# Two layers and a third sum over a graph: one group of every second pass of the third sum counted by source node on TensorE, and ScalarE's tile of each last full pass gathered

## The chip, the cores and the metric

The kernel runs on 1 core of one Trainium2 chip. The time is that of the device in microseconds (us). The kernel before took 9507.16 us, the median of 3 runs (9503.04 to 9524.47).

## The reference, cut to what matters

There are 12500 nodes with 128 features, and 212500 edges (100000 random ones in both directions and one self loop for each node), sorted by destination. Each edge has one of 8 relations. Three sums over the edges follow each other, each on the rows that the one before made possible:

```python
def rgcn(x, W, SW, b):                       # W: 8 matrices of 128 x 128
    msg = einsum('nd,rde->rne', x, W)[rel, src]
    return relu(segment_sum(msg, dst) + x @ SW + b)
x1 = layernorm(x + rgcn(rgcn(x, w1, sl1, b1), w2, sl2, b2))      # sums one and two
feat = relu(x1 @ W1 + b1)
h = feat * d_invsqrt                          # d_invsqrt from the in-degrees
agg = segment_sum(h[src], dst)                # sum three: no relation, no matrix
out = layernorm(x1 + (feat - agg * d_invsqrt) @ W2 + b2)
```

What is computed in sum three is, for each destination node n, the sum over its edges of the row h[src]. The result is 12500 x 128 in float32.

## The kernel before, in words

The edge list is cut into 1661 tiles of 128 edges (a tile has one edge for each of the 128 partitions). Seven tiles (KG) are a group, and since the edges are sorted by destination, a group's destinations lie in a window of GN = 64 nodes. Two groups are a pair, and four pairs (p = 0 to 3), so 56 tiles, are a pass, i. There are IT = 29 full passes (0 to 28) and a rest of 37 tiles in three pairs (LEFT) in each sum.

For a tile, the 128 source rows (512 bytes each) are brought into the tile `rows`, which has room for one pass. Three engines do this. GpSimd takes 54 of the 56 tiles with one indirect DMA each (L808). SyncE and ScalarE bring one tile each, the last two of pair 3 (`OWN`), with one small DMA for each of the 128 rows (L867), whose addresses they load 16 at a time from a list in SBUF (`load_own`, L863); the list itself is fetched each pass (L846). In pass 0 ScalarE's tile is gathered by GpSimd too.

TensorE then adds up a group: in sum three one matmul for each tile, of the rows by a one-hot matrix S of 128 x 64 that VectorE makes from the destinations (`one_hot`, L1228), into PSUM (L1211; float32, which is two weight loads and two matmuls for each tile). VectorE adds the 64 columns to the accumulator `acc` (L1255). In sums one and two the one-hot also tells the relation, and a mix with the 8 matrices follows (L980).

The order is tied together so. TensorE ends a pair and raises `summed`. ScalarE's `take` (L771) waits for it, copies the next pass's indices of that pair, and GpSimd may gather them. In a pass of ScalarE (`indices_and_own`) the order in its one queue is: its rows of lists 1 to 3 (48 rows), `take` of pair 0, 32 rows, `take` of pair 1, 32 rows, `take` of pair 2, `take` of pair 3, the wait for the end of the pass on TensorE (`own_free`), and the 16 rows of the next pass's list 0. SyncE's tile of a pass may begin when TensorE has ended the pass before, since it uses the same place in `rows`; then come its 128 rows.

When the sums of 512 nodes are complete (25 chunks in 29 passes), the chunk's tail is run at the end of the pass (`Tail3`): TensorE multiplies (L1708), VectorE normalizes, with a square root on ScalarE between (L1718, which waits for VectorE's variance, and VectorE's next instruction waits for the root, L1748), and SyncE loads (L1288) and stores (L1693) rows and waits for the store. The tail stands in each engine's queue between two passes. Loops run on the engines with register values; the passes belonging to a chunk come from a table.

In the places that the change touches: `Gathers.run` (GpSimd's passes), `wait_rows` (TensorE's waits), `indices_and_own` (ScalarE), `plain_sum` (sum three) and the tiles of `Tail3`.

## Time and profile before

| | us |
|---|---|
| median of 3 runs | 9507.16 |
| the profiled execution's own time | 9512.93 |
| span of its profile, first to last instruction | 9511.2 |
| GpSimd's gathers of sum three (L808), busy | 1504.7 |
| TensorE's matmuls of sum three (L1211), busy | 745.3 |
| VectorE, busy over all | 1975.7 |

Busy times are those of an engine's own instructions; instructions that only issue a DMA, load a register, branch or wait are not counted as busy. A line of a timeline gives the start, the length of a merged stretch of like instructions, the engine, line, operation and operands, how many they were, and in brackets how long the engine had been idle and what ended that. SPq and ACTq are the DMA issues of SyncE and ScalarE, PEld are TensorE's weight loads. Sum three runs from about 6497 us to the end.

### The profile page before, as it was taken

Reading aid. Unit: us, or ns where it says so; the run is one execution under the profiler, and the core shown is the slowest. Engines: PE = TensorE matmul, PEld = TensorE weight load, DVE = VectorE, ACT = ScalarE, POOL = GpSimd, SP = SyncE. Lnnn points to the kernel's source line nnn. Section 1 sums busy time; section 2 is a strip of 40 time slices with the busy share of each in tenths; the row PEclk is TensorE's granted clock in tenths of the full one; section 3 lists DMA queues with packets and bytes.
Section 4 is the critical chain, followed back from the end, with each engine's and each line's share of the span. In section 5 each row is a group of like instructions: output and inputs, shape, how many; then the busy total and the mean of one; then the engine's idle time right before and its main releaser. Section 6 shows DMA issues by size and latency. Waiting matters only on the chain.

```text
span 9511.2 us, 99977 instructions
## 1 busy us (share of the span) xinstructions
PE 3350.8 (35%) x13625; PEld 2381.6 (25%) x13626; DVE 1975.7 (21%) x3147; ACT 130.3 (1%) x430; POOL 4561.2 (48%) x4822
## 2 busy tenths in 40 slices
PE   3333433434333434344343343344222222222223
PEld 2222222222222322222222222224222222222223
DVE  4322332323232212122121221122001001001001
ACT  0000000000000000000000000000000000000000
POOL 4545444444444444444544444444554454455454
PEclk6666666666666666666666666665555555555555
DMA  1111111111111111111111111111111111111111
GB/s 49 40 40 42 36 38 40 41 39 39 38 43 41 36 40 44 40 40 42 40 47 40 40 41 40 46 42 35 40 42 39 40 42 40 37 43 41 37 43 39
DMA packets 239445, 385.74 MB, mean 41 GB/s; under 512 B 106473, under 2 KB 137532, under 8 KB 239100
## 3 DMA queue, kind: packets, MB, share of 16 engines
q0 software_dynamic: 153984, 315.67, 12.7%
q1 hardware_dynamic: 61768, 60.65, 2.1%
q10 hardware_dynamic: 23348, 6.44, 0.3%
q14 instruction: 326, 2.67, 0.1%
q8 instruction: 19, 0.31, 0.0%
HBM read 356.60 MB, written 25.75 MB: 40 GB/s over the span
## 4 chain that ended last, share of the span: by engine, by line
SPq 49%; issue 37%; ACTq 8%; PE 3%; DMA 1%; DVE 1%; another core or an unknown queue 0%; ACT 0%; DVEq 0%
SPq L867 38%; ACTq L867 7%; SPq L863 6%; ACTq L863 1%; PE bank L1008 1%; SPq L684 1%; SPq L686 1%; SPq L846 1%; SPq L683 1%; PE bank L980 0%; SPq L109 0%; SPq L850 0%; SPq L856 0%; PE bank L1565 0%
## 5 line engine op out<-in xcount | busy, mean ns | idle before, releaser
L808 POOL DMA_INDIRECT rows<-x_d,idx x1590 | 1504.0, 946 | 1687.7 <-ACT idx L771 1202.7
L808 POOL DMA_INDIRECT rows<-in_x_dram,idx x1604 | 1518.1, 946 | 1651.4 <-ACT idx L771 1186.7
L808 POOL DMA_INDIRECT rows<-h_d,idx x1583 | 1504.7, 951 | 1505.4 <-ACT idx L771 1026.0
L1008 PE MATMUL bank<-r_S,rows 128*128 128x128 f32 x6644 | 1115.6, 331 | 2023.5 <-DMA rows<-in_x_dram 998.4
L1008 PEld LDWEIGHTS bank<-r_S,rows 128*128 128x128 f32 x6644 | 1058.0, 242 | 2083.9 <-issue 2062.0
L1211 PE MATMUL bank<-r_S,rows 128*128 128x64 f32 x3322 | 745.3, 411 | 2093.9 <-DMA rows<-h_d 1479.7
L1211 PEld LDWEIGHTS bank<-r_S,rows 128*128 128x128 f32 x3322 | 733.6, 328 | 2108.1 <-issue 2107.4
L1104 DVE COPY r_agg<-bank 128x512 f32<-128x512 f32 x476 | 320.5, 687 | 2969.1 <-PE bank L1008 2059.7
L1255 DVE TENSOR_TENSOR acc<-acc,bank 128x64 f32 x238 | 52.7, 222 | 2093.2 <-issue 962.4
L1046 DVE TENSOR_TENSOR r_S<-bank,key 128x1792 f32<-128x1792 f32 x238 | 479.0, 2013 | 0.7 <-issue 0.7
L980 PE MATMUL bank<-r_agg,w1s 128*128 128x512 f32 (+1 forms) x512 | 448.5, 1044 | 42.5 <-DVE r_agg L1104 24.1
L980 PE MATMUL bank<-r_agg,w2s 128*128 128x512 f32 (+1 forms) x512 | 448.3, 1044 | 35.2 <-DVE r_agg L1104 21.3
L992 PE MATMUL bank<-zeros_bf 128*128 128x512 bf16 x476 | 223.5, 470 | 594.3 <-DVE r_agg L1104 483.8
L1044 DVE TENSOR_REDUCE r_placed<-r_hot 128x192 bf16<-128x1344 bf16 x119 | 291.0, 2445 | 4.1
L1090 DVE TENSOR_TENSOR acc<-acc,bank 128x64 f32 x476 | 105.7, 222 | 799.6 <-issue 352.9
L992 PEld LDWEIGHTS bank<-zeros_bf 128*128 128x128 bf16 x476 | 52.6, 110 | 674.2 <-DVE r_agg L1104 506.7
L980 PEld LDWEIGHTS bank<-r_agg,w1s 128*128 128x128 f32 x512 | 122.8, 251 | 323.9 <-issue 323.6
L980 PEld LDWEIGHTS bank<-r_agg,w2s 128*128 128x128 f32 x512 | 123.4, 253 | 315.9 <-issue 315.6
L1041 DVE TENSOR_TENSOR r_hot<-bank,b_spot 128x1344 bf16<-128x1344 f32 x119 | 185.3, 1557 | 18.2 <-issue 6.3
L771 ACT COPY idx<-src_i 128x14 int32 x360 | 72.6, 203 | 7419.9 <-issue 6032.1
L1361 PE MATMUL bank<-ident,d_zr 128*128 128x128 f32 x98 | 27.5, 435 | 321.5 <-DVEq L1636 321.5
L1228 DVE TENSOR_TENSOR r_S<-bank,key 128x896 f32<-128x896 f32 x119 | 129.8, 1092 | 35.8 <-DVE acc L1255 27.7
(157 smaller groups left out, 1357.9 us busy)
## 6 DMA issues: line engine op xcount, KB each, us to landing
rows<-in_x_dram SPq DMA_DIRECT2D x3712, 0.5 KB
rows<-x_d SPq DMA_DIRECT2D x3712, 0.5 KB
rows<-h_d SPq DMA_DIRECT2D x3712, 0.5 KB
rows<-in_x_dram ACTq DMA_DIRECT2D x3584, 0.5 KB
rows<-x_d ACTq DMA_DIRECT2D x3584, 0.5 KB
rows<-h_d ACTq DMA_DIRECT2D x3584, 0.5 KB
rows<-in_x_dram,idx POOLq DMA_INDIRECT x1604
rows<-x_d,idx POOLq DMA_INDIRECT x1590
```

The lines of the kernel that those rows point to most:

```text
L808: pool.indirect_dma_start(out=self.c.rows[:, self.place(s), :], out_offset=None, in_=self.table[:, :], in_offset=bass.IndirectOffsetOnAxis ...
L863: _, starts = nc.values_load_multi_w_load_instructions(c.list_i[o][0:1, first:first + LIST], engines=bass.OrderedEngineSet([eng.engine]), ...
L867: eng.dma_start(to[row:row + 1, :], table[bass.ds(start, ROW)].unsqueeze(0)).then_inc(self.own[o][row // (P // OWN_SEMS)], 16)
L980: mm = pe.matmul(mix_ps[:, 0:groups * GN], W[:, r, :], agg[:, h0:h0 + groups, :, r], start=(r == 0), stop=(r == NREL - 1))
L992: pe.matmul(agg_ps[j][:, :], c.zeros_bf[:, :], c.zeros, start=True, stop=False, skip_group_check=True)
L1008: mm = pe.matmul(agg_ps[j][:, bass.ds(offs[j * KG + k], TK)], c.rows[:, g.place(h * KG + k), :], S[:, pb, j * KG + k, :], start=False, sto ...
L1041: ch.then(dve.tensor_tensor(hot[:, b, :, :], spots.unsqueeze(1).broadcast_to([P, PT, SPOTS]), bc_last(blocks.spot[:, at], SPOTS), ALU.is_e ...
L1044: dve.tensor_reduce(placed[:, b, :, :], hot[:, b, :, :].rearrange("p (j k) n -> p j n k", k=KG), AX.X, ALU.add)
L1046: dve.tensor_tensor(S[:, b, :, :], c.iota[:, :].unsqueeze(1).broadcast_to([P, PT, TK]), bc_last(c.key[:, at], TK), ALU.is_equal).then_inc( ...
L1104: dve.tensor_copy(agg[:, h, :, :], agg_ps[h % BUFS][:, :].rearrange("p (n r) -> p n r", r=NREL)).then_inc(agg_out, 1)
L1211: mm = pe.matmul(sum_ps[b][:, j * GN:(j + 1) * GN], c.rows[:, g.place(h * KG + k), :], S[:, b, j * KG + k, :], start=(k == 0), stop=(k == ...
L1228: dve.tensor_tensor(S[:, p % BUFS, :, :], c.iota[:, 0:GN].unsqueeze(1).broadcast_to([P, PT, GN]), bc_last(c.key[:, bass.ds(i * UN + p * PT ...
```

## The change

In every even pass from 2 to 28 of sum three, group 6 (`DENSE`, the first group of pair 3, 7 tiles) is no longer gathered. In its place the table h (12544 rows with padding, 6.4 MB) is kept in SBUF, loaded by 13 DMAs at the start of the sum from ScalarE's queue. It is cut into 13 units of 1024 rows (the last has 256). For a unit, VectorE makes a one-hot of the place of each edge's source within the unit (`pair_hot`, 128 x 896, bf16) and TensorE multiplies it with a one-hot of the partition (`part_hot`), which counts, for each source row of the unit and each of the 64 destinations, how many edges there are (`count`: one matmul of zeros and 7 of bf16, into a PSUM bank of 512 columns). VectorE copies the counts out, and TensorE multiplies the unit's 8 blocks of table rows with them (`mult`: 8 float32 matmuls of 128 x 64, the counts read with a stride of 8), all into one bank, `dense_ps`, which VectorE adds to the accumulator in place of the gathered group. The 26 steps on TensorE (`PE_ENDS`) and 27 on VectorE (`DVE_ENDS`) for one such group are spread over the two passes before its place: after the pairs 0 to 3 of the odd pass (4, 4, 4 and 3 steps on TensorE, 7, 4, 4 and 3 on VectorE), and after pairs 0 to 2 of the even pass (4, 4 and 3; 4, 4 and 1). GpSimd's loop of sum three holds two passes, an odd and an even one.

In all three sums, ScalarE brings no rows in the last full pass (28); its tile is gathered by GpSimd. The tiles `key` and `relf` are bf16. `Tail3`'s tiles share room. Sum three takes its number of rounds and its table of windows from the same entry as the others.

The diff, cut to its core:

```diff
+DENSE = RING - 2
+DENSE_TILES = range(DENSE * KG, DENSE * KG + KG)
...
+def ends_of(i):
+
+    return (i + (ENDING - (IT - 1))) >> ENDING_BITS
...
-            iteration(q, 0, FULL, skip, first=True)
-            with pool.Fori(1, IT) as i:
-                iteration(q, i, FULL)
+            iteration(q, 0, FULL, skip, OWN[:BY_ACT])
+            if self.then:
+                with pool.Fori(1, IT - 1) as i:
+                    iteration(q, i, FULL, others=OWN)
+                iteration(q, IT - 1, FULL, others=OWN[:BY_ACT])
+            else:
+                with pool.Fori(0, IT // 2 - 1) as n:
+                    i = pool.snap(n * 2)
+                    iteration(q, i + 1, FULL, others=OWN)
+                    iteration(q, i + 2, FULL, others=(*DENSE_TILES, *OWN))
+                iteration(q, IT - 2, FULL, others=OWN)
+                iteration(q, IT - 1, FULL, others=(*DENSE_TILES, *OWN[:BY_ACT]))
             iteration(q, IT, LEFT)
...
-                pe.wait_ge(self.landed[h], i * (gathered * 16) + (gathered + 1) * 16)
+                pe.wait_ge(self.landed[h], i * (gathered * 16) + ends_of(i) * 16 + (gathered + 1) * 16)
...
-    with act.If(i > 0):
+    with act.If(i > ends * IT):
         g.load_own(nc, act, BY_ACT, own[:-4])
+    act.end_ifs()
+    with act.If(i > IT - 2):
+        g.list_there(act, BY_ACT, q, i)
+        for share in g.own[BY_ACT]:
+            act.sem_inc(share, P // OWN_SEMS * 16)
     act.end_ifs()
     for p in range(PR):
         g.take(act, p, q, i + 1)
         if p < PR // 2:
-            with act.If(i > 0):
+            with act.If(i > ends * IT):
                 g.load_own(nc, act, BY_ACT, own[-4:][2 * p:2 * p + 2])
             act.end_ifs()
         if p == PR // 2:
             g.fetch_list(act, BY_ACT, i + 1)
-    with act.If(i < IT - 1):
+    with act.If(i < IT - 2):
...
+        for u in range(UNITS):
+            act.dma_start(table[:, u * NREL:u * NREL + rows_of(u), :],
+                          g.table[u * AT_UNIT:u * AT_UNIT + P * rows_of(u), :].rearrange("(p r) f -> p r f", r=rows_of(u))
+                          ).then_inc(table_in, 16)
...
+            def dense(half, np, p, before):
+
+                made = steps_before(q, half, DVE_STEPS)
+                _, offs = nc.values_load_multi_w_load_instructions(
+                    c.off_i[0:1, bass.ds(half * (2 * PR) + DENSE // PAIR, 1), 0:KG], engines=bass.OrderedEngineSet([pe.engine]),
+                    min_val=0, max_val=(GN - TN) * NREL, skip_runtime_bounds_check_because="clamped on the chip")
+                order = [(count_done(u), 0, u) for u in range(UNITS)] + [(mult_done(u), 1, u) for u in range(UNITS)]
+                for _, kind, u in sorted(order)[part(PE_ENDS, p, before)]:
+                    if kind == 0:
+                        pe.wait_ge(from_dve, made + hot_done(u))
+                        pe.matmul(count_ps[u % 2][:, :], c.zeros_bf[:, :], c.zeros, start=True, stop=False,
+                                  skip_group_check=True)
+                        for k in range(KG):
+                            mm = pe.matmul(count_ps[u % 2][:, bass.ds(offs[k], TK)], part_hot[:, k, :],
+                                           pair_hot[u % 2][:, k, :], start=False, stop=(k == KG - 1),
+                                           skip_group_check=True)
+                    else:
+                        pe.wait_ge(from_dve, made + copy_done(u))
+                        if u == 0:
+                            pe.wait_ge(added, np + BUFS)
+                            pe.wait_ge(table_in, UNITS * 16)
+                        of = counts[u % 2].rearrange("p (n r) -> p n r", r=NREL)
+                        for r in range(rows_of(u)):
+                            mm = pe.matmul(dense_ps, table[:, u * NREL + r, :], of[:, :, r],
+                                           start=(u == 0 and r == 0), stop=(u == UNITS - 1 and r == LAST_ROWS - 1))
+                    mm.then_inc(from_pe, 1)
...
+                        if h == DENSE:
+                            def gathered(to):
+                                for k in range(KG):
+                                    pe.matmul(to, c.rows[:, g.place(h * KG + k), :], S[:, b, j * KG + k, :],
+                                              start=(k == 0), stop=(k == KG - 1))
+                                gate(pe, c.passed)
+
+                            with pe.If(i < 1):
+                                pe.wait_ge(g.landed[h], KG * 16)
+                                gathered(dense_ps)
+                            pe.end_ifs()
+                            with pe.If(i < half * 2):
+                                pe.wait_ge(g.landed[h], i * (KG * 8) + KG * 24)
+                                gathered(sum_ps[b][:, j * GN:(j + 1) * GN])
+                            pe.end_ifs()
+                            continue
...
+                    if part is FULL:
+                        with pe.If(i < half * 2):
+                            dense(half, np, p, True)
+                        pe.end_ifs()
+                        if p < DENSE // PAIR:
+                            with pe.If(i > (half * 2 - i) * IT):
+                                dense(half, np, p, False)
+                            pe.end_ifs()
...
+            order = [(1, 0, 0)] + [(hot_done(u), 1, u) for u in range(UNITS)] + [(copy_done(u), 2, u) for u in range(UNITS)]
+            for _, kind, u in sorted(order)[part(DVE_ENDS, p, before)]:
+                if kind == 0:
+                    tiles = bass.ds(half * (2 * UN) + DENSE_TILES[0], KG)
...
+                    ins = dve.scalar_tensor_tensor(part_hot[:, :, :], iota, float(NREL), bc_last(at, P),
+                                                   ALU.mult, ALU.is_equal)
+                elif kind == 1:
+                    if u >= 2:
+                        dve.wait_ge(from_pe, done + count_done(u - 2))
+                    ins = dve.scalar_tensor_tensor(pair_hot[u % 2], iota, float(u * AT_UNIT), bc_last(spot[:, :], TK),
+                                                   ALU.add, ALU.is_equal)
+                else:
+                    dve.wait_ge(from_pe, done + count_done(u))
+                    ins = dve.tensor_copy(counts[u % 2], count_ps[u % 2][:, :])
+                ins.then_inc(from_dve, 1)
+
+        per_table = 5 + window_steps(None)
...
+                            with dve.If(i > half * 2 - 1):
+                                dve.tensor_tensor(window, window, dense_ps, ALU.add).then_inc(steps, 1)
+                            dve.end_ifs()
```

## Rows read from the trace of the kernel before

**Rows 1.** The page, part 4: the chain that ended last, by line.

```profile
SPq L867 38%; ACTq L867 7%; SPq L863 6%; ACTq L863 1%; PE bank L1008 1%; SPq L684 1%; SPq L686 1%; SPq L846 1%; SPq L683 1%; PE bank L980 0%; SPq L109 0%; SPq L850 0%; SPq L856 0%; PE bank L1565 0%
```

**Rows 2.** Timeline of SyncE's queue, 8000 to 8210 us: start, length, engine, line, operation, count.

```profile
8042.21 0.38 SPq L1693 DMA_DIRECT2D out_dram<-d_o  x1
...
8066.81 76.59 SPq L867 DMA_DIRECT2D rows<-h_d  x128
...
8144.44 0.38 SPq L1693 DMA_DIRECT2D out_dram<-d_o  x1
```

**Rows 3.** Groups of POOL instructions by line; then the timeline, 8000 to 8120 us.

```profile
L808 POOL DMA_INDIRECT rows<-h_d,idx x1583 | 1504.7, 951 | 1505.4 <-ACT idx L771 1026.0 <-issue 479.4
...
8098.77 0.94 POOL L808 DMA_INDIRECT rows<-h_d,idx  x1 [26.86 <-ACT idx L771]
```

**Rows 4.** SyncE's rows in four windows: 7999:8012.6, 8042:8071.9, 8076:8098 and 8098.7:8116.

```profile
7999.07 14.09 SPq L867 DMA_DIRECT2D rows<-h_d  x14
...
8066.81 6.30 SPq L867 DMA_DIRECT2D rows<-h_d  x3
...
8076.01 22.14 SPq L867 DMA_DIRECT2D rows<-h_d  x57
...
8098.56 16.55 SPq L867 DMA_DIRECT2D rows<-h_d  x21
```

**Rows 5.** Busy time by window, PE, PEld, DVE, ACT, POOL, granted clock, DMA share, GB/s.

```profile
8072.00:8098.50 26.50, 14.22 (x65) 14.16 (x65) 5.90 (x14) 0.27 (x2) 0.00 (x0) 0.50 0.02 5
```

**Rows 6.** Timeline of ScalarE and its queue, 8000 to 8210 us.

```profile
8045.07 25.25 ACTq L867 DMA_DIRECT2D rows<-h_d  x16
8071.77 0.30 ACT L1718 ACTIVATE d_sd<-d_mv,eps 128x4 f32<-128x4 f32 x1 [28.08 <-issue]
8078.76 18.53 ACTq L867 DMA_DIRECT2D rows<-h_d  x48
...
8120.88 19.39 ACTq L867 DMA_DIRECT2D rows<-h_d  x32
```

**Rows 7.** Timeline of TensorE, 8036 to 8150 us.

```profile
8048.47 8.15 PE L1211 MATMUL bank<-r_S,rows 128*128 128x64 f32 x37 [0.39 <-issue]
8057.76 0.27 PE L1211 MATMUL bank<-r_S,rows 128*128 128x64 f32 x1 [1.13 <-issue]
...
8078.80 11.33 PE L1211 MATMUL bank<-r_S,rows 128*128 128x64 f32 x52 [0.21 <-issue]
8144.52 1.08 PE L1211 MATMUL bank<-r_S,rows 128*128 128x64 f32 x4 [54.39 <-DMA rows<-h_d]
```

**Rows 8.** Timeline of VectorE, 8036 to 8150 us.

```profile
8050.88 0.38 DVE L1765 BATCH_NORM_AGGREGATE d_mv<-d_st 128x2 f32<-128x6 f32 x4
...
8076.71 0.58 DVE L1255 TENSOR_TENSOR acc<-acc,bank 128x64 f32 x2 [3.28 <-remote]
```

**Rows 9.** Groups by line, shapes kept apart.

```profile
L1104 DVE COPY r_agg<-bank 128x512 f32<-128x512 f32 x476 | 320.5, 687 | 2969.1 <-PE bank L1008 2059.7 <-remote 702.2 <-issue 206.9
L1228 DVE TENSOR_TENSOR r_S<-bank,key 128x896 f32<-128x896 f32 x119 | 129.8, 1092 | 35.8 <-DVE acc L1255 27.7 <-issue 7.3 <-PE bank L1211 0.6
L980 PE MATMUL bank<-r_agg,w1s 128*128 128x512 f32 x464 | 436.4, 1109 | 26.8 <-issue 18.5 <-DVE r_agg L1104 8.3
L992 PE MATMUL bank<-zeros_bf 128*128 128x512 bf16 x476 | 223.5, 470 | 594.3 <-DVE r_agg L1104 483.8 <-issue 110.1
```

**Rows 10.** DMA queues, 700 to 910 us (sum one); then line L867, first and last start.

```profile
q14 instruction: 20, 0.16, 0.3%
...
L867 SPq DMA_DIRECT2D rows<-in_x_dram x3712: 2/225/1403, 112.7 to 3163.8; - x196
```

**Rows 11.** The end of the span: timeline of TensorE, 9470 to 9512 us.

```profile
9477.26 1.09 PE L1211 MATMUL bank<-r_S,rows 128*128 128x64 f32 x4 [55.27 <-DMA rows<-h_d]
...
9491.12 9.91 PE L1211 MATMUL bank<-r_S,rows 128*128 128x64 f32 x46
```

**Rows 12.** The chain that ended last, the whole span, in order of time.

```profile
8042.21 2.88 DMA out_dram<-d_o
```

129 lines of the change are left out of this document (111 added, 18 removed).

## The prediction

> **What bounds the kernel now.** Read first the chain that ended last: SyncE's own rows (L867) are 38% of the span, ScalarE's 7%, TensorE's matmuls hardly anything [rows 1]. So the length of a pass is that of 128 row loads, not of 54 gathers. SyncE's queue shows one pass of sum three: a store, 128 rows in 76.6 us, the next store; from store to store 102.2 us [rows 2]. The rows end at 8143.4 and TensorE's last matmuls of the pass begin at 8144.5, after 54 us of idleness [rows 7]. ScalarE's rows end at 8120.9 + 19.4 = 8140.3, 3.1 us earlier [rows 6]. GpSimd has 26.9 us of idleness in this pass, waiting for ScalarE's `take` [rows 3].
>
> By that alone fewer gathers would bring nothing. The second thing to see is how fast SyncE gets on. While GpSimd gathers nothing it issues 57 rows in 22.1 us, 0.39 us each; in the 17 us after a pause of GpSimd 21 rows in 16.6 us, 0.79 each, or 14 in 14.1 us, 1.0 each; deep in the long stretch of pairs 2 and 3 together (26 gathers), 3 rows in 6.3 us, 2.1 each [rows 4, 5]. TensorE shows the same: 37 matmuls in 8.2 us, then one in about 2.8 us by the record until GpSimd ends, then 52 in 11.3 [rows 7]; ScalarE needs 25.3 us for 16 rows and later 18.5 for 48 [rows 6]. Whatever the way, gathering holds up every other queue, and the more the longer it lasts. A gather that goes away is thus worth something although GpSimd idles.
>
> **The gathers removed.** 14 even passes lose 7 gathers each, at (1504.7 + 479.4) / 1583 = 1.25 us [rows 3], 8.8 us, out of the long stretch. They run right after TensorE has ended the odd pass before, where all is slowest. In 8.8 us at 2.1 us a row SyncE issues 4 rows; when GpSimd is silent these take 4 x 0.39 = 1.6 us. If all engines shift along, a pass with its long stretch cut gets 8.8 - 1.6 = 7.2 us shorter: 14 x 7.2 = 101 us, the upper end.
>
> The lower end comes from ScalarE. Its square root (L1718) came at 8071.8, because its own 16 rows held it until 8070.3, though the variance had been there since 8051.3 [rows 6, 8]. After an odd pass VectorE and TensorE now first have a piece of the new work in their queues (3 steps: mult 5, count 7, mult 6), and the chunk's tail comes behind it. A mult is 8 float32 products, 16 pairs of load and matmul; 37 took 8.15 us, 0.22 each [rows 7], so 3.5 us (the matmul of 512 strided columns takes 1.11 us [rows 9], 64 columns at most an eighth of it, so the load sets the pace). A count is one matmul of zeros, 0.47 us [rows 9], and 7 bf16 matmuls of 128 columns, which no row shows: between a quarter of 0.47 us and 0.22 us plus a load of 0.2, so 1.3 to 3.4 us with the zeros; I take 2. The piece is then 3.5 + 2 + 3.5 = 9 us at full speed, and it moves the variance from 9 us to some 18 to 28 us after the end of the pass (the late end if VectorE's queue is in its slow phase). The root can now come at 20.5 us instead of 29.5. If the variance comes at 28, ScalarE gains 1.5 us, its rows end as before, and SyncE's lead moves no more than the 3.1 us by which ScalarE is ahead today: 14 x 3.1 = 43 us. Between 3.1 and 7.2 I take 6, nearer the upper, since half of that range of the variance is early enough: -84 us.
>
> **The work added on TensorE.** A group costs 13 counts and 12.25 mults: 13 x 2 + 12.25 x 3.5 = 69 us for two passes, beside 2 x 56 x 2 x 0.22 = 49 us of gathered tiles, all at the granted clock of 0.50 (1.2 GHz) that sum three shows [rows 5]; should the busier engine be granted 2.4 GHz, these get shorter, which I leave out. TensorE idles 54 us at the end of each pass [rows 7], so its busy time fits. The odd pass is the tight one. VectorE only gets to pair 0 some 34.5 us after the end of the pass before (8076.7 against 8042.3) [rows 8], and the first count needs its one-hots, some 14 small operations and three of 896 elements at 1.09 us [rows 9]: +8 us. From 43 us on: piece 0 (9.5 us), pair 1 (6), piece 1 (11), pair 2 (6), piece 2 (11), pair 3 (5): 91 us, against the last rows at 102. Ten us of cover. But from 56 us on GpSimd gathers again, and from there TensorE has about 370 instructions to go. After a long wait it issued some 140 before it was slowed [rows 7]. With such a stock in each of the two short stretches, and full speed in the pause of 4.5 us, it ends at about 100 us, just in time. I charge 1 us for each odd pass: +14 us. Without that cover each late us is a us of the pass. In the even pass 300 instructions are left at that point: earlier.
>
> VectorE: 13 x (1.09 + 0.69) + 1.09 + 14 x 0.2 = 27 us for two passes [rows 9], beside idleness of 58 us a pass: nothing, but for the root's delay above. The two conditional branches a pair on both engines: some 10 register instructions, hidden in fast time.
>
> **The table.** 6.4 MB by ScalarE's queue at the start. A store of 0.26 MB takes 2.9 us to land [rows 12], so at that pace some 71 us. ScalarE has no rows in pass 0, and the first mult is in pass 1. What it does to SyncE's first rows and the first gathers no row shows: between 0 and 20 us; I take +5.
>
> **ScalarE's tile in the last full pass.** ScalarE then has only its takes to do, and GpSimd starts the rest's gathers when it otherwise idles, 18 us earlier. SyncE loses fast time: of its 128 rows 3 come before, 20 in the 8 us that remain fast, 21 in the next 17 us, 13 in the last 29 us of a stretch of 37 gathers, and 71 behind it, 28 us: 112 us instead of 102, +10. In return nothing is gathered any more after the pass: today 46 matmuls begin at 9491.1, 14 us after the last rows of the pass at 9477.3 [rows 11], and most of that goes, -8 to -12. Where ScalarE was the late one (ACTq's 7% in [rows 1]) it gains more. Three times this: between -30 and +20, I take 0. bf16 in `key` reads fewer bytes at the same element rate in the one-hots: 0, between -5 and +5.
>
> **The sum.** 9512.9 (the profiled execution's own time) - 84 + 14 + 5 + 0 = 9448; that execution stood 5.8 us over the median of 9507.2, so 9442.
>
> A rule against the change, in sentences that the rest can do without: in sum one's passes the queue of instruction fetches moves 20 packets in 210 us [rows 10], the loops there not staying on chip. The Trainium skill, "Runtime: NRT & Kernel Launch", section "Instruction fetch mechanics", says that fetch is sequential and that a taken branch to outside the resident window stalls for a DMA. Sum three's loop grows by about 700 instructions on TensorE and by branches, so by this rule it would pay at each pass; by [rows 4, 7], where the slow stretches come and go with GpSimd alone, it would not.
>
> **The rivals.**
> - TensorE late (slower). Place: the odd passes, its queue between 56 and 102 us. If its stock is not refilled in the pause, it gets, like SyncE, some 45 instructions per short stretch [rows 4], 370 don't end by 102, and GpSimd's pair 2 of the next pass begins at 99 and slows the rest. It decides from the point where the gathered tiles of pair 3 end later than 102 us. Price: 30 us at the worst, 12 likely, in 14 passes, +168, and the even passes keep half their gain, -42: 9507 + 168 - 42 - 0 = 9630. For it: SyncE's slow rate straight after a pause. Against: TensorE's 37 pairs at full speed when GpSimd had been gathering for 9 us.
> - ScalarE decides: -43 instead of -84, 9483; with a point lost to the odd passes, no change.
> - All shift fully and TensorE is never late: -101 + 5: 9411.
> - Loops leave the on-chip window: sum one's passes, with such fetches, take (3163.8 - 112.7) / 29 = 105.2 us [rows 10], sum three's 102.2; with some margin 4 us in 28 passes, +112, beside the -84 + 14 + 5: 9555.
> - The slow phase isn't GpSimd's doing but comes with TensorE's own work at the end of a pass; the shorter stretch frees nothing: 9505 to 9530. Against it, ScalarE's and SyncE's rate fall in every stretch, also with TensorE idle.
>
> **How the numbers follow.** Forecast 0.35, full shift 0.10, ScalarE decides 0.15 (of it 0.05 within 0.2%), TensorE late 0.28, loops 0.05, nothing freed 0.07. A measurement of this kernel tells 0.2% (19 us) from no change. Faster 0.35 + 0.10 + 0.10 = 0.55; within 0.2% 0.12; slower 0.33. Range: from 9380 (-84 with the last passes at -30) to 9620, which leaves out the worse half of TensorE's case; the forecast's own range is 9400 to 9480.
>
> **What would show it.** Right: periods of SyncE's stores alternate, about 102 after odd starts and 96 when the 19-gather stretch is in; 7 gathers fewer in 14 passes; TensorE idle at least a few us before its last matmuls in odd passes, ended by a DMA. Wrong: that wait gone, and rows of SyncE ended long before; or L1718 as late as before, with ScalarE's last row after SyncE's. Sum three alone carries the change; sums one and two within 15 us.

## The result, and the profile after

The changed kernel took 9622.88 us (median of 4 runs, 9604.95 to 9631.23) against 9514.52 us (9503.04 to 9524.47) for the kernel before: 1.0109 of its time, 95% interval 1.0094 to 1.0123. It is slower by about 105 us. I had forecast 9442 and a range to 9620, so the sign is wrong and the time lies just outside the range.

Sum three begins and ends nearly as before (its pass 0 is over at 6611 against 6609 us; from the last rows to the last instruction it takes 38 against 35 us). Nearly the whole loss is in the passes of sum three. I take the end of a pass to be the later of SyncE's and ScalarE's last row. Then a pass lasted 102.6 us before in the mean, the even and the odd ones alike. After, the even passes last 103.5 and the odd ones 109.2 us. A pair of passes went from 205.3 to 212.7 us, and 14 x 7.4 = 104 us. I use these pair lengths below. Within a pass, the medians for ScalarE's square root (called the root) and for its 48 rows are counted as in the prediction, from TensorE's last matmuls of the pass before, about 1 us behind that pass' last row.

The kernel after, part 4 of the page, the chain that ended last by engine and by line (L893 are now the rows of SyncE and ScalarE):

```profile
issue 35%; SPq 27%; ACTq 26%; PE 5%; another core or an unknown queue 4%; DVE 2%; DMA 1%; DVEq 0%; ACT 0%
SPq L893 21%; ACTq L893 21%; ACTq L889 3%; SPq L889 3%; PE bank L1034 1%; PE bank L1342 1%; PE bank L1773 1%; PE bank L1006 0%; DMA rows<-x_d 0%; PE bank L1781 0%; SPq L696 0%; DMA rows<-h_d 0%; SPq L872 0%; PE bank L1920 0%
```

Before, SyncE had 38% for its rows and ScalarE 7% [rows 1]. Now they have 21% each. The chain has moved to ScalarE, TensorE's products have little of it. ScalarE's queue in the kernel after, two passes (start, length, engine, line, operation, count, in brackets idleness and what ended it; L1930 is the square root, L788 a `take`):

```profile
7455.23 14.08 ACTq L893 DMA_DIRECT2D rows<-h_d  x16
7470.76 0.30 ACT L1930 ACTIVATE d_sd<-d_mv,eps 128x4 f32<-128x4 f32 x1 [16.91 <-issue]
7490.76 19.01 ACTq L893 DMA_DIRECT2D rows<-h_d  x48
7510.41 0.20 ACT L788 COPY idx<-src_i 128x14 int32 x1 [39.35 <-PE bank L1342]
7511.78 22.84 ACTq L893 DMA_DIRECT2D rows<-h_d  x32
7534.93 0.20 ACT L788 COPY idx<-src_i 128x14 int32 x1 [24.32 <-issue]
7536.29 22.96 ACTq L893 DMA_DIRECT2D rows<-h_d  x32
...
7562.35 0.20 ACT L788 COPY idx<-src_i 128x14 int32 x1 [2.58 <-PE bank L1342]
7563.95 17.86 ACTq L893 DMA_DIRECT2D rows<-h_d  x16
7594.07 0.30 ACT L1930 ACTIVATE d_sd<-d_mv,eps 128x4 f32<-128x4 f32 x1 [31.53 <-DVEq L1957]
7599.58 19.10 ACTq L893 DMA_DIRECT2D rows<-h_d  x48
7619.34 0.20 ACT L788 COPY idx<-src_i 128x14 int32 x1 [24.97 <-issue]
7620.70 22.88 ACTq L893 DMA_DIRECT2D rows<-h_d  x32
7643.90 0.20 ACT L788 COPY idx<-src_i 128x14 int32 x1 [24.36 <-issue]
7645.25 21.72 ACTq L893 DMA_DIRECT2D rows<-h_d  x32
```

Two things are new against [rows 6]. In the second pass shown, the one behind an odd pass, the 16 rows are through at 7581.8, yet the root waits for VectorE until 7594.07; before, it was the other way round. And 32 rows take 22.8 us here, against 19.39 in the row shown before. In the medians the two stretches of 32 rows took 20.1 and 20.3 us before; now they take 23.0 and 22.9 in odd passes, 22.9 and 21.3 in even ones. SyncE's queue in the same two passes, kernel after:

```profile
7455.02 102.54 SPq L893 DMA_DIRECT2D rows<-h_d  x128
...
7558.59 0.38 SPq L1905 DMA_DIRECT2D out_dram<-d_o  x1
7564.76 0.77 SPq L872 DMA_DIRECT2D list_i<-own_d  x1
7569.20 78.56 SPq L893 DMA_DIRECT2D rows<-h_d  x128
...
7649.94 0.79 SPq L1905 DMA_DIRECT2D out_dram<-d_o  x1
```

In the pass with the shorter gathering SyncE has its rows out at 7647.8, 19 us before ScalarE (7667.0): the gain that I forecast for SyncE is there, and nobody can use it. Behind that pass comes an odd one, where the full stretch of 26 gathers is in again. There SyncE is slowed as well, and not only ScalarE: in the median it begins its rows 20 us earlier than in the kernel before (it was through early with the even pass), and yet ends them 105.8 us after the last row of the pass ahead, against 103; ScalarE ends at 107.7. Where SyncE begins so early, its 128 rows mostly take 101 to 103 us. In the kernel before, in the four passes in which it begins as early, they took 95. One of them, kernel before:

```profile
7121.20 94.75 SPq L867 DMA_DIRECT2D rows<-h_d  x128
```

Where the root was held: VectorE (first block) and TensorE (second block) in the kernel after, from the end of the odd pass on TensorE at 7562 us:

```profile
7564.47 0.68 DVE L1410 COPY w1s<-bank 128x512 f32<-128x512 f32 x1
7565.06 1.08 DVE L1406 SCALAR_TENSOR_TENSOR w2s<-bank,r_spot 128x896 bf16<-128x896 f32 x1
7587.48 0.69 DVE L1410 COPY w1s<-bank 128x512 f32<-128x512 f32 x1 [21.34 <-remote]
...
7593.60 0.38 DVE L1977 BATCH_NORM_AGGREGATE d_mv<-d_st 128x2 f32<-128x6 f32 x4
```

```profile
7561.57 0.66 PE L1342 MATMUL bank<-r_S,rows 128*128 128x64 f32 x2 [1.98 <-DMA rows<-h_d]
7563.12 3.67 PE L1310 MATMUL bank<-w1s,r_table 128*128 128x64 f32 x16 [0.90 <-issue]
7566.60 0.62 PE L1297 MATMUL bank<-zeros_bf 128*128 128x512 bf16 x1
7567.02 0.95 PE L1300 MATMUL bank<-w2s,r_part_hot 128*128 128x128 bf16 x7
7567.76 3.62 PE L1310 MATMUL bank<-w1s,r_table 128*128 128x64 f32 x16
7588.56 2.24 PE L1920 MATMUL bank<-gw2s,d_work 128*128 128x128 f32 x8 [17.18 <-DVE d_work L1945]
```

The sizes are as forecast: 3.6 us for a mult (I had 3.5), 1.4 for a count (2), the piece 8.3 us (9), over at 7571.4. The count that VectorE's copy L1410 waits for is ready at 7568. The copy begins at 7587.48, 19.5 us later; GpSimd's stretch of gathers ended at 7584. The variance (L1977) is there 34.7 us after the last row (7559.3). In the median, counted from TensorE's last matmuls, it came at 33.5 us; I had let it lie between 18 and 28.

TensorE's last matmuls of an odd pass waited for the rows, as in the row at 7561.57, but with little to spare: in nine of the 14 odd passes it had been idle for 2.3 us or less, where it was 51 to 56 us before. At the end of three even passes (2, 16 and 22) TensorE was late itself. In pass 22 the last row was issued at 8937.5, and the last 30 matmuls of the pass were still to come. TensorE, kernel after:

```profile
8938.69 0.66 PE L1342 MATMUL bank<-r_S,rows 128*128 128x64 f32 x2 [12.75 <-issue]
8940.02 6.23 PE L1342 MATMUL bank<-r_S,rows 128*128 128x64 f32 x28 [0.67 <-issue]
```

The odd passes behind these three took 110.5 to 115.4 us, against 107.8 in the median, together some 17 us more. The gathers and the two kinds of products over the whole run, kernel after (groups of instructions: busy us, mean ns, idleness before them):

```profile
L825 POOL DMA_INDIRECT rows<-h_d,idx x1486 | 1406.2, 946 | 1687.3 <-ACT idx L788 1233.9
...
L1310 PE MATMUL bank<-w1s,r_table 128*128 128x64 f32 x2744 | 611.9, 395 | 166.3 <-issue 132.7
```

97 gathers fewer (98 removed, one added) took 98.5 us off GpSimd's busy time [rows 3] and put 182 us on its idleness.

### The profile page after: what moved, and what is told of

It reads as the page before. It is cut to its first block, busy times and chain, and to the rows that moved or that the text cites. A ratio compares the mean times of both kernels' runs of the same rounds, so it can differ in the third digit from the quotient of the medians.

```text
span 9616.1 us, 110744 instructions
## 1 busy us (share of the span) xinstructions
PE 4078.3 (42%) x17629; PEld 3041.9 (32%) x17630; DVE 2318.4 (24%) x3723; ACT 130.2 (1%) x430; POOL 4464.1 (46%) x4727
## 3 DMA queue, kind: packets, MB, share of 16 engines
q0 software_dynamic: 150944, 309.44, 12.3%
## 4 chain that ended last, share of the span: by engine, by line
issue 35%; SPq 27%; ACTq 26%; PE 5%; another core or an unknown queue 4%; DVE 2%; DMA 1%; DVEq 0%; ACT 0%
SPq L893 21%; ACTq L893 21%; ACTq L889 3%; SPq L889 3%; PE bank L1034 1%; PE bank L1342 1%; PE bank L1773 1%; PE bank L1006 0%; DMA rows<-x_d 0%; PE bank L1781 0%; SPq L696 0%; DMA rows<-h_d 0%; SPq L872 0%; PE bank L1920 0%
## 5 line engine op out<-in xcount | busy, mean ns | idle before, releaser
L825 POOL DMA_INDIRECT rows<-h_d,idx x1486 | 1406.2, 946 | 1687.3 <-ACT idx L788 1233.9
L1034 PEld LDWEIGHTS bank<-r_S,rows 128*128 128x128 f32 x6644 | 1051.5, 240 | 2064.3 <-issue 2042.8
L1342 PE MATMUL bank<-r_S,rows 128*128 128x64 f32 x2916 | 652.6, 407 | 645.6 <-DMA rows<-h_d 376.6
L1342 PEld LDWEIGHTS bank<-r_S,rows 128*128 128x128 f32 x2916 | 630.7, 321 | 663.9 <-issue 663.2
L1310 PE MATMUL bank<-w1s,r_table 128*128 128x64 f32 x2744 | 611.9, 395 | 166.3 <-issue 132.7
L1310 PEld LDWEIGHTS bank<-w1s,r_table 128*128 128x128 f32 x2744 | 590.7, 321 | 173.7 <-issue 133.2
L1018 PE MATMUL bank<-zeros_bf 128*128 128x512 bf16 x476 | 222.5, 467 | 613.3 <-DVE r_agg L1130 489.5
L1297 PE MATMUL bank<-zeros_bf 128*128 128x512 bf16 x182 | 110.2, 606 | 463.2 <-DVE w2s L1406 457.4
L1410 DVE COPY w1s<-bank 128x512 f32<-128x512 f32 x182 | 124.7, 685 | 366.3 <-remote 314.0
```

Of the source, the lines that this page charges most:

```text
L825: pool.indirect_dma_start(out=self.c.rows[:, self.place(s), :], out_offset=None, in_=self.table[:, :], in_offset=bass.IndirectOffsetOnAxis ...
L1018: pe.matmul(agg_ps[j][:, :], c.zeros_bf[:, :], c.zeros, start=True, stop=False, skip_group_check=True)
L1034: mm = pe.matmul(agg_ps[j][:, bass.ds(offs[j * KG + k], TK)], c.rows[:, g.place(h * KG + k), :], S[:, pb, j * KG + k, :], start=False, sto ...
L1310: mm = pe.matmul(dense_ps, table[:, u * NREL + r, :], of[:, :, r], start=(u == 0 and r == 0), stop=(u == UNITS - 1 and r == LAST_ROWS - 1))
L1342: mm = pe.matmul(sum_ps[b][:, j * GN:(j + 1) * GN], c.rows[:, g.place(h * KG + k), :], S[:, b, j * KG + k, :], start=(k == 0), stop=(k == ...
L1410: ins = dve.tensor_copy(counts[u % 2], count_ps[u % 2][:, :])
```

## The experiments

Each kernel ran beside the kernel before on the same chip; ratios are to that one, with 95% intervals.

### One part alone

The tile of the last full pass alone, from the kernel before:

```diff
+            iteration(q, IT - 1, FULL, others=OWN[:BY_ACT])
...
-    with act.If(i > 0):
+    with act.If(i > ends * IT):
```

> The kernel before with one part of the change alone: ScalarE's tile of each last full pass is gathered by GpSimd. In the changed kernel's trace sum three's passes carry about 101 us of the 108 us loss, so whichever theory holds, this part is worth little. Theory (ScalarE decides the passes of sum three, the added work does it): within 15 us of the kernel before, passes of sum three 102 to 103 us as before, the last full pass of sums one and two 5 to 10 us longer and what follows it shorter by as much. Rival (the last passes carry the loss): 30 us or more over the kernel before.

1.0026 [1.0016, 1.0036]. That is about 25 us over the kernel before by the ratio, more than the 15 us of my theory and less than the 30 us of its rival. The three last full passes lasted 112.7, 115.1 and 123.5 us, against 107.6, 113.4 and 102.8 before, together +27.5. The prediction's 0 fails by the end: from sum three's last rows to the last instruction it took 34 us, before 35. SyncE's queue in this kernel shows the last pass (128 rows; the row before it is the pass ahead):

```profile
9347.77 78.31 SPq L876 DMA_DIRECT2D rows<-h_d  x128
...
9447.86 101.67 SPq L876 DMA_DIRECT2D rows<-h_d  x128
```

Its rows took 23 us longer beside the merged gathers (I had +10), and nothing came back. In the changed kernel the three passes differ otherwise (112.6, 109.8 and 100.8), so the 25 us can't simply be carried over.

The gathers removed alone, and as a rival the same number removed from a place where SyncE is fast:

```diff
+                    iteration(q, i + 1, FULL)
+                    iteration(q, i + 2, FULL, left_out=range(6 * KG, 6 * KG + KG))
```

> The kernel before, with group 6 of the even passes 2 to 28 of sum three not gathered and nothing put in its place (TensorE adds up the rows that stood there, so this group's sums are not the reference's). It prices the removed gathers alone. Theory (a shorter long stretch lets all queues shift along when no work is added): 7.2 us less in each of 14 pairs of passes, 100 us under the kernel before, the square root L1718 about 9 us earlier after odd passes. Rival (ScalarE's rows don't follow, SyncE's 3 us lead is all): 43 us under. Rival (gathers hold nobody up): no change.

> The kernel before, with group 0 instead of group 6 left out of the gathers of the even passes of sum three (its sums are then not the reference's). The 7 gathers go from a short stretch, at whose time the queues issue a row in 0.8 to 1 us, instead of from the end of the long one at 2.1 us a row. Theory (a gather is worth what it holds up): 3 to 5 us less in each of 14 passes, 40 to 70 us under the kernel before, about half of what e2 gave (1.36%). Rival (each gather is worth its 1.25 us wherever it stands): as e2, 1.2% or more. Rival (ScalarE's in-order rows hide it): nothing.

Group 6 left out (its sums are then incomplete): 0.9864 [0.9848, 0.9881], -122 us of 9539; the even pass fell to 94.3 us, the odd stayed at 102.8. Group 0 left out: 0.9880 [0.9864, 0.9897], -113 us. The first holds and is even exceeded: 122 / 14 = 8.7 us for each shortened pass, above my upper end of 7.2. The second missed its own expectation: gathers removed outside the long stretch were worth as much. Removing a gather was thus worth 1.15 to 1.25 us in both places, about the 1.25 us that it takes, and the "long stretch" is not what made it dear. ScalarE's queue with group 6 left out, behind an odd pass whose last rows came at 7909.7:

```profile
7913.84 21.23 ACTq L873 DMA_DIRECT2D rows<-h_d  x16
7935.36 0.30 ACT L1727 ACTIVATE d_sd<-d_mv,eps 128x4 f32<-128x4 f32 x1 [22.90 <-remote]
7938.52 18.85 ACTq L873 DMA_DIRECT2D rows<-h_d  x48
7957.83 0.20 ACT L771 COPY idx<-src_i 128x14 int32 x1 [22.17 <-issue]
7959.20 20.79 ACTq L873 DMA_DIRECT2D rows<-h_d  x32
```

Here is what the change should have looked like: the root 25.7 us after the last row, the 48 rows 28.8 us after it. In the medians, counted from TensorE's last matmuls, the root came at 24.7 us here (29.3 in the kernel before) and at 33.6 in the changed kernel, the 48 rows at 27.9 and at 39.1.

The work alone: the changed kernel with group 6 gathered as well, its rows then unused.

```diff
-                    iteration(q, i + 2, FULL, others=(*DENSE_TILES, *OWN))
+                    iteration(q, i + 2, FULL, others=OWN)
```

> The changed kernel with group 6 gathered in the even passes as well (the rows are then not used): it prices the added work alone. Theory (the added work costs about 15 us for two passes, partly as the root's delay behind the piece at the end of odd passes, partly as slower rows of ScalarE while GpSimd gathers and TensorE and VectorE work): 9690 to 9730, that is 70 to 110 over the changed kernel, and ScalarE's stretches of 32 rows take 22 to 23 us instead of 20. Rival (in the changed kernel the 7 gathers were hidden and their removal bought nothing): within 20 us of the changed kernel.

1.0206 [1.0189, 1.0223], +204 us, with the tile's part in it. A pair of passes lasted 220.2 us. So the removed gathers are worth 220.2 - 212.7 = 7.5 us with the work in place and 206.4 - 197.1 = 9.3 us without it (206.4 is the pair on that chip, by the kernel with the tile alone), and the work costs 13.8 (without the removal) to 15.6 us a pair, 190 to 220 us in 14 pairs. These pairs are of single executions on different chips; by the ratios to the kernel before, the removal is worth 6.6 to 8.7 us and the work 12.3 to 15 us a pair, 170 to 210 us in all. I had charged 14 us in all.

### Parts of the work

No piece behind pair 3 of the odd pass (its steps go behind the earlier pairs), and the same without the tile's part, on two chips:

```diff
-    PE_ENDS, DVE_ENDS = (0, 4, 8, 12, 15, 19, 23, PE_STEPS), (0, 7, 11, 15, 18, 22, 26, DVE_STEPS)
+    PE_ENDS, DVE_ENDS = (0, 5, 10, 15, 15, 19, 23, PE_STEPS), (0, 8, 13, 18, 18, 22, 26, DVE_STEPS)
```

> The changed kernel with the steps that stood behind pair 3 of the odd pass moved ahead of it (5, 5 and 5 steps behind pairs 0 to 2 of the odd pass, none behind pair 3). Theory (this piece holds up the chunk's tail, and with it ScalarE's root and rows, in the slow stretch): after odd passes the root comes 8 to 10 us earlier, these passes get 8 to 10 us shorter, 100 to 140 us under the changed kernel, about 9500. Rival (TensorE is late before its last matmuls of odd passes): slower than the changed kernel by 20 us or more, since odd passes get 3 more steps. Rival (only the slower rows count): within 20 us of the changed kernel.

> The changed kernel without the piece behind pair 3 of odd passes (as in e4) and without ScalarE's tile of the last full passes given to GpSimd. Theory (the tile's part costs 25 to 30 us by itself, and adds to the rest): 20 to 35 us under e4, so 0.1 to 0.3% over the kernel before. Rival (the two parts don't add, since with the dense group the last pass of sum three ends early anyway): within 10 us of e4.

> The kernel of e7 again (the change without the piece behind pair 3 of odd passes and without the tile of the last passes). Where the kernel before takes 9500 to 9700: as e7, within 0.1% of it. Where it takes about 6070 and GpSimd decides: the 3 last passes have 1.25 us less of gathers each, but ScalarE's rows in them; theory: 1.4 to 1.8% faster, as the change itself (g1, 1.6%), so that this version would lose nothing on one chip and gain as much on the other. Rival: without the tile's part the ends of the sums cost 10 to 20 us more there, 1.3% or less.

Without the piece 1.0048 [1.0032, 1.0064]; without the tile's part as well 1.0004 [0.9994, 1.0013] and, on the other chip, 1.0019 [1.0009, 1.0028]. Without the piece the root comes at 27.0 instead of 33.6 us and the 48 rows begin at 32.5 instead of 39.1; the even pass falls to 99.8 us, the odd one stays at 109.5. So the piece is worth about 60 us, by 1.0109 against 1.0048, half of what I had expected, and the tile about 30 to 40. Without both, the change loses 0 to 0.2%, but nothing of the -122 is left.

What keeps the odd passes long is then SyncE: without both parts they took 110.4 and 110.1 us on the two chips, and SyncE's last row came 3.7 us behind ScalarE's. It began its rows about as late after the pass before as in the kernel before (23 to 27 us), and its 128 rows took 85 to 87 us, where they took 79 before.

Far fewer matmuls in the same steps (one of 7 in a count, one of 8 in a mult; the sums of that group are not complete), with everything else of the change:

```diff
-                        for k in range(KG):
+                        for k in range(KG - 1, KG):
...
-                        for r in range(rows_of(u)):
+                        for r in range(1):
```

> The changed kernel with all steps and waits, but 1 of 7 bf16 matmuls in each count and 1 of 8 products in each mult (the group's sums are left incomplete). It asks which of the added instructions slow ScalarE's stretches of 32 rows, 22.9 us in the changed kernel, 20.2 before. Theory (TensorE's instructions beside a gathering GpSimd): 20.5 us again, and the root after odd passes comes with the piece's few matmuls, at about 25 us instead of 33.6; odd passes some 5 us shorter, even ones some 8: 150 to 190 us under the changed kernel. Rival (VectorE's instructions, or the branches on all queues): the stretches stay at 22.5 us or more and only the root's part goes, 40 to 80 us.

0.9986 [0.9977, 0.9996]. By the ratios that is 119 us better than the changed kernel, twice what taking out the piece brought, and between my theory (150 to 190) and its rival (40 to 80). A pair lasted 207.5 us on a chip where everything is slower: by the kernel before's 9663 us, less 6700 for the first two sums, a pair of it takes some 209 us here (an estimate). The 48 rows behind an odd pass begin at 31.8 us, as without the piece. ScalarE's two stretches of 32 rows in an odd pass, here:

```profile
7591.77 23.49 ACTq L893 DMA_DIRECT2D rows<-h_d  x32
...
7616.93 20.87 ACTq L893 DMA_DIRECT2D rows<-h_d  x32
```

In the medians of odd passes they take 23.4 and 20.9 us. In the changed kernel it was 23.0 and 22.9, and without the piece and the tile's part, on the same chip, 23.1 and 23.3. So without the bulk of TensorE's matmuls the second stretch is 2 us shorter, nearly as before the change. The first is as slow as with it: that comes with what is left, VectorE's steps, the waits, the branches and fewer matmuls.

Is it many short instructions? The kernel before with 64 matmuls of 16 columns more on TensorE, in each pass where it is otherwise idle beside the gathers; and as the rival 16 matmuls of 512 columns:

```diff
+                            if part is FULL and h == RING - 1 and k == KG - len(OWN):
+                                gate(pe, c.passed)
+                                pe.wait_ge(g.idx_ready, (q * (IT + 1) + i + 1) * PR + 1)
+                                for n in range(64):
+                                    pe.matmul(c.psum[7][:, 0:16], c.zeros_bf[:, :], c.zeros_bf[:, 0:1].broadcast_to([P, 16]),
+                                              start=True, stop=True)
```

> The kernel before with 64 short bf16 matmuls of 16 columns (128 instructions, some 6 to 8 us busy) on TensorE in each full pass of sum three, issued when ScalarE has taken pair 0 of the next pass, so at the start of a stretch of gathers in which TensorE did nothing. Theory (every queue's instructions use up a stock that all share while GpSimd gathers): ScalarE's first stretch of 32 rows goes from 20.2 to 22 to 24 us, passes get 2 to 4 us longer, 50 to 110 us over the kernel before. Rival (queues don't disturb each other): within 15 us of it.

> The same place, but 16 long bf16 matmuls of 512 columns (32 instructions, some 7.5 us busy). Theory (the number of instructions counts, not the busy time): about a quarter of what f4 costs, under 25 us over the kernel before, and 32 rows in 20.2 to 21 us. Rival (TensorE's busy time or reads count): as much as f4 or more.

> The kernel of f4 and g3 a third time, in the hope of a chip with slowed queues. Where the kernel before takes 9500 to 9700: theory (a limit shared by the queues) ScalarE's first stretch of 32 rows in 22 to 24 us instead of 20.2, the second in 20 to 21, 50 to 110 us over the kernel before; rival (queues don't disturb each other) within 15 us. Where it takes about 6070: 0.1% over, as f4 and g3.

The chip of the first two was of another kind (below) and showed nothing: 1.0012 [1.0002, 1.0022] and 1.0007 [0.9996, 1.0018]. On a chip like that of the result the 64 cost 1.0060 [1.0040, 1.0080], +57 us. ScalarE's queue there:

```profile
7931.89 22.35 ACTq L867 DMA_DIRECT2D rows<-h_d  x32
7954.55 0.20 ACT L771 COPY idx<-src_i 128x14 int32 x1 [23.80 <-issue]
7955.91 20.54 ACTq L867 DMA_DIRECT2D rows<-h_d  x32
```

And TensorE's added matmuls of that pass:

```profile
7930.80 1.87 PE L1214 MATMUL bank<-zeros_bf 128*128 128x16 bf16 x64 [8.11 <-ACT idx L771]
```

They are over in 1.9 us, just where the gathers of the next pass and the first 32 rows begin. These take 22.35 us, the second 32, without such matmuls, 20.54. A pass gets 2 us longer, and 28 times this are the 57. SyncE is still the last by 2.8 us, and its 128 rows took 80 to 81 us in the medians, against 78 to 79 in the kernel before: the added matmuls slow both queues, although they share no data with them. The few long ones were not run on such a chip, so number and length are not told apart.

VectorE's work left out (its steps only wait and signal; the group's sums are wrong by that):

```diff
-                    ins = dve.tensor_copy(counts[u % 2], count_ps[u % 2][:, :])
-                ins.then_inc(from_dve, 1)
+                gate(dve, c.passed)
+                dve.sem_inc(from_dve, 1)
```

> The changed kernel with VectorE's 27 steps of the added work kept as waits and increments only, without their operations (the group's sums are then wrong); TensorE does all its matmuls. ScalarE's stretches of 32 rows took 20.2 us before, 22.9 in the changed kernel and still 23.2 with few matmuls on TensorE. Theory (it is the number of instructions in the queues beside a gathering GpSimd, whosever they are, and TensorE's pairs of tiles that the waits for VectorE push into that time): the stretches get a little shorter, 21.5 to 23, since TensorE no longer waits and does more of its work before GpSimd begins; 20 to 70 us under the changed kernel. Rival (VectorE's operations themselves disturb, by their accesses): 20.3 us, as before the change, 100 us or more under it.

> The kernel of f3 again (VectorE's added operations left out, waits and increments kept), since the chip of f3 doesn't show the slow queues. Where the kernel before takes 9500 to 9700: theory (number of instructions of all queues beside GpSimd) 32 rows in 21.5 to 23 us, 20 to 70 us under the changed kernel; rival (VectorE's operations themselves) 20.3 us, 100 us or more under it. Where it takes about 6070: as f3, 1.5% under the kernel before, and by 0 to 0.3% under or over the changed kernel.

0.9850 [0.9833, 0.9866] and 0.9840 [0.9820, 0.9860], but both on chips of the other kind, where the change itself gives as much. VectorE's share of the slowing stays open.

### A pause for GpSimd

If gathering holds up the other queues, GpSimd's idleness is worth something in the right place. The kernel before, with 5 memsets of about 1.1 us on GpSimd ahead of pair 3's gathers, in sum three:

```diff
+                if self.turns == 2 and part is FULL and p == PR - 1:
+                    for n in range(PAUSE):
+                        pool.memset(self.c.pause[:, :], 0.0).then_inc(self.c.paused, 1)
+                        pool.wait_ge(self.c.paused, (q * IT + i) * PAUSE + (n + 1))
+                        gate(pool, self.c.passed)
```

> The kernel before with a pause of GpSimd (5 memsets of 1024 columns, some 5 us) between pairs 2 and 3 of each full pass of sum three. It tests whether the other queues are slow because the stretch of 26 gathers is long, or only because gathers are in progress. Theory (each queue has a stock that a pause refills): ScalarE's 16 rows and its root end about 8 us earlier, some of the 48 rows are issued in the second half, passes get 3 to 6 us shorter, 80 to 150 us under the kernel before. Rival (every us of gathering costs the same): the end of the gathers moves 5 us, passes get up to 5 us longer or stay.

0.9869 [0.9853, 0.9885]: 9536.25 against 9663.43 us, with every gather still done. A pair lasted 199.1 us, against the estimate of 209 for the kernel before on this chip (the profiled execution was the fastest of its four, by 24 us). ScalarE's queue with the pause:

```profile
7983.94 12.97 ACTq L875 DMA_DIRECT2D rows<-h_d  x16
7997.20 0.30 ACT L1726 ACTIVATE d_sd<-d_mv,eps 128x4 f32<-128x4 f32 x1 [14.64 <-issue]
8000.38 28.91 ACTq L875 DMA_DIRECT2D rows<-h_d  x48
8029.75 0.20 ACT L774 COPY idx<-src_i 128x14 int32 x1 [32.25 <-issue]
```

In the 6 us of silence the 16 rows end, the tail runs through to the root, and the 48 rows begin in the median at 20.0 us instead of 36.6; then they run beside the gathers, in 28.9 us instead of 18.5, and still end 7 us earlier. Of the kernels with complete sums this is the fastest on chips of this kind: both the kernel before and the change lose to it. Then the pause in all sums' passes (the diff is against the kernel with the pause), on a chip of the other kind, the first that came up:

```diff
-                if self.turns == 2 and part is FULL and p == PR - 1:
+                    if part is FULL and h in PAUSES and not (isinstance(i, int) and i == 0):
```

> The kernel before with a pause of GpSimd of some 6 us (5 memsets) between groups 5 and 6 of each full pass from 1 to 28 in all three sums. In sum three alone it gave 1.3%. Theory (the root and 48 rows of ScalarE start in the second half of the gathers): sum one's passes get 3 to 4 us shorter as well; sum two's, whose ScalarE is the last by other waits (its tail has a longer chain on VectorE and TensorE), 0 to 3: 2.2 to 3.5% under the kernel before. Rival (it only helps where the tail is as short as sum three's): 1.2 to 1.5%.

1.0784 [1.0766, 1.0802], 6539 against 6066 us, 5.6 us for each of 84 pauses: where the passes are bound by GpSimd itself, each pause is paid in full. What it would bring in sums one and two on a chip of the first kind was not seen.

### The change on a chip of the other kind

> The changed kernel itself, on the chip of this group. The kernel before took 9507 to 9663 us in three groups of runs and 6066 in the one of f1, f3, f4 and f5: there no queue is slowed beside GpSimd, ScalarE's 32 rows take 12 us and GpSimd gathers without a pause, 54 times 1.25 = 67.5 us a pass. Theory, if the kernel before takes about 9500 to 9700 here: ScalarE decides, 0.8 to 1.3% slower. Theory, if it takes about 6070: GpSimd decides, and the 98 gathers less are worth 122 us less what the rest of the pass gives back: 1.3 to 2% faster. Rival: the added work costs time there as well, within 0.5% of the kernel before.

The unchanged copy of the changed kernel ran at 5973.66 against 6071.28 us: 0.9839 [0.9819, 0.9859]. It is faster there, by 98 us; 97 gathers of 1.25 us fewer are 121. SyncE's queue in that run:

```profile
5027.55 50.25 SPq L893 DMA_DIRECT2D rows<-h_d  x128
...
5078.83 0.38 SPq L1905 DMA_DIRECT2D out_dram<-d_o  x1
5084.34 0.30 SPq L872 DMA_DIRECT2D list_i<-own_d  x1
5090.60 50.28 SPq L893 DMA_DIRECT2D rows<-h_d  x128
```

128 rows in 50.3 us, 0.39 each, wherever GpSimd stands. By a kind of chip I mean no more than this difference, which a group of runs showed or didn't: the record gives chip number 0 to a group of either kind, so whether it is the chip or a state of it that differs is open. Part 4 of that run's page, by line:

```profile
POOL rows L825 31%; ACTq L893 17%; ACTq L889 5%; PE bank L1006 5%; PE bank L1310 3%; PE bank L1034 2%; PE bank L1342 2%; PE bank L1300 1%; PE bank L1920 1%; PE bank L1773 1%; DMA rows<-x_d 1%; DVE acc L1116 1%; PE bank L1781 1%; DVE d_st L1973 1%; SPq L893 1%
```

GpSimd leads the chain, and a pair of passes lasts 130.8 us, near its 101 gathers (126). The two kernels with added matmuls once more, beside it:

> The kernel of f4 again (the kernel before with 64 short matmuls on TensorE at the start of pair 0's gathers). Where the kernel before takes 9500 to 9700: theory (a stock shared by the queues) 32 rows of ScalarE in 22 to 24 us instead of 20.2, 50 to 110 us over the kernel before; rival (queues don't disturb each other) within 15 us. Where it takes about 6070: as f4, 0.1% over.

> The kernel of f5 again (16 long matmuls in the same place). Where the kernel before takes 9500 to 9700: theory (the number of instructions counts) under 25 us over the kernel before, 32 rows in 20.2 to 21 us; rival (busy time or reads count) as much as g3 or more. Where it takes about 6070: as f5, no difference.

1.0006 [0.9993, 1.0019] and 0.9998 [0.9986, 1.0009]: on this kind of chip added instructions hold up nobody.

## Why the prediction was wrong

- **What bounds the kernel: right.** SyncE's 128 rows, with ScalarE's just ahead of them, and every queue held up beside the gathers. The -122 us of the removal alone, the -127 us of the pause with all gathers in place, and the other kind of chip, where rows take 0.39 us beside gathers, agree.
- **The gathers removed (-84): their worth was there, the way through ScalarE was not.** Removing them alone brought 122 us (I took 84, at most 101). But the forecast counted on "The root can now come at 20.5 us instead of 29.5". It came at 33.6, later than before, and even with nothing added at 24.7: the piece was priced at full speed plus some delay, and VectorE's copy behind it began only when GpSimd's stretch was over. Without the piece the root came at 27.0. So the rival "ScalarE decides" held here, with the sign that I had named for a wrong forecast, ScalarE's last row behind SyncE's, by 18.2 us in the median of the even passes and 1.9 in that of the odd ones.
- **The work added on TensorE (+14): the step that failed.** "I charge 1 us for each odd pass" stands against 12 to 16 us a pair, 170 to 220 us in all. I looked for the cost where TensorE is late, and that is the smaller part: the ten us of cover in odd passes were 2.3 us or less in most, and TensorE was late at the end of three even passes, for some 17 us. What I left out is that the added work holds up ScalarE's and SyncE's rows. Against the removal alone the even pass lost 103.5 - 94.3 = 9.2 us, for ScalarE's 48 rows began 11.2 us later. The odd pass lost 109.2 - 102.8 = 6.4 us: ScalarE's rows of such a pass ended 7.3 us later than before, 1.9 of it ahead of the two stretches of 32 rows and 5.4 in them. This second term was not in the sum at all. SyncE's rows are slower too (102.5 us against 95 from an equally early start), and where ScalarE is no longer in the way, SyncE alone keeps the odd pass at 110 us. Of ScalarE's 5.4 us some 2 go with most of TensorE's matmuls, in the second stretch; 64 short matmuls bring 2 us in the first by themselves.
- **VectorE's "idleness of 58 us a pass: nothing"** fails with it, as far as the root is concerned; its part in the slower rows is open.
- **The table (+5): right.** Sum three's pass 0 ended 2 us later than before.
- **The last pass' tile (0): +25 when done alone,** just over the upper end of +20. The end gave back 1 us and not 8 to 12.
- **Two slips in the working** change nothing here: 9507 + 168 - 42 is 9633, and the range's 9380 comes from the full shift of -101 with the last passes at -30 (with -84 it would be 9412).

**The rivals.** "TensorE late" gave the nearest number (9630) mostly by the wrong way: in the odd passes, where it put the loss, the last matmuls waited for rows. That the number is near is luck. "Loops leave the on-chip window" had its sign and not its price. The queue of instruction fetches in the two passes shown (7440 to 7660 us: packets, MB, share), kernel after:

```profile
q14 instruction: 10, 0.08, 0.1%
```

The kernel before has none in sum three's passes. The kernel without piece and with the tile's part fetches as often (20 packets in 400 us), the one without both practically never. Their ratios are 1.0048 against 1.0004 and 1.0019, that is 28 to 42 us, and the longer last passes of the tile's part are in them. So the fetches cost at most 3 us a pair, and not the 8 of that rival. The Trainium skill's rule in "Runtime: NRT & Kernel Launch", "Instruction fetch mechanics", names the fetches rightly; the stall that it tells of is small here, or hidden.

**What would show it.** SyncE's stores do alternate, but mostly by 90 to 93 and 119 to 124 us, and not by 96 and 102. Of sums one and two, the end of the second moved by 1 us.

**What stays open.** Why a queue is held up beside the gathers, and by what added instructions hold it up further, no row shows. Nor is it told apart how much of the slower rows is VectorE's, the branches' or the short matmuls' doing, and why chips differ. Of the 4.6 us by which the 48 rows without the piece still begin later than with the removal alone (32.5 against 27.9), 3 are TensorE's: it ends the odd pass later, and ScalarE's 16 rows begin 7.1 us after the last row instead of 4.1; the rest is open. A finer pause, or the change with a pause, was not tried.

## What to carry to other kernels

When the queue that sets the pace is one that others slow down, work put on idle engines is not free: take one run with the work added and nothing removed, and one with the removal alone, before building both. If one engine's work holds up the others, a deliberate pause in it at the point where a short chain is waiting can be worth as much as taking work off it (1.3% here, against 1.4% for 98 gathers fewer), and does harm where that engine is the bound. And if a chain of short steps hangs on an engine's queue, new work goes behind that chain, not ahead of it.

## What the runs showed of the hardware

- The same kernel took 9507 to 9663 us in some groups of runs and 6066 to 6071 us in others, each group on one chip. In the first, SyncE's rows take 0.39 us when GpSimd is silent and up to 2.1 us when it gathers; in the others 0.39 always. GpSimd's gather is 0.95 us on both. The change costs 1.1% on the one and brings 1.6% on the other.
- 64 matmuls of 16 columns that nobody waits for, over in 1.9 us, made ScalarE's 32 row DMAs 2 us longer and SyncE's 128 about as much, beside gathers.
- 7 gathers fewer in every second pass brought 122 us in one place and 113 in another: what counted was their number.
